# Two graph-attention layers: the column maximum and the raw scores spread by way of memory, and a third of the normalising moved to GpSimd

## The reference

```
h     = relu(layernorm(x))
Wh    = h @ W                              # 1024 x 128
e1,e2 = Wh @ a1, Wh @ a2                   # one number per node each
e     = leaky_relu(e1[i] + e2[j], 0.2)     # 1024 x 1024
att   = softmax over j of e where adj[i, j] > 0
out   = att @ Wh                           # layer 0: elu(out)
x     = x + out
```

## Time and profile before

| | us |
|---|---|
| median of 3 runs | 290.95 (290.85 to 292.67) |
| the profiled execution | 291.18 |
| its span | 289.4 |
| TensorE busy | 285.1 (99%) |
| VectorE busy | 254.4 (88%) |
| ScalarE busy | 195.1 (67%) |
| GpSimd busy | 79.7 (28%) |

### The profile page before, as it was taken

The page is one execution under the profiler, slowest core; times in us unless marked ns, Lnnn a source line. Parts: engine busy times, 40 slices in busy tenths (PEclk is TensorE's granted clock), DMA queues, the critical chain, the costliest instruction groups (busy, mean ns, idle before and its releaser), DMA issues.

```text
span 289.4 us, 6600 instructions
## 1 busy us (share of the span) xinstructions
PE 285.1 (99%) x2523; PEld 284.2 (98%) x2523; DVE 254.4 (88%) x493; ACT 195.1 (67%) x534; POOL 79.7 (28%) x143
## 2 busy tenths in 40 slices
PE   7999999999999999999999999999999999999996
PEld 7999999999999999999999999999999999999995
DVE  3898899898989989898998979979797997779986
ACT  4686795995959679495886929569292865916400
POOL 2412705315071420706035070512407042000000
PEclk9999999999999999999999999999999999999999
DMA  7999659597795949679287896959769596896922
GB/s 235 418 407 407 243 183 408 216 371 298 260 413 163 415 170 359 278 245 412 76 315 286 291 378 204 404 186 389 294 243 410 166 409 250 313 406 205 374 104 75
DMA packets 25387, 84.52 MB, mean 292 GB/s; under 512 B 3966, under 2 KB 5132, under 8 KB 25356
## 3 DMA queue, kind: packets, MB, share of 16 engines
q1 hardware_dynamic: 24780, 83.70, 76.8%
q10 hardware_dynamic: 576, 0.39, 0.4%
HBM read 79.83 MB, written 4.26 MB: 291 GB/s over the span
## 4 chain that ended last, share of the span: by engine, by line
PE 99%; POOL 0%; DVE 0%; issue 0%; POOLq 0%
PE acc L1041 76%; PE prj L957 9%; PE tp L887 5%; PE acc L1056 2%; PE acc L876 2%; PE acc L937 1%; PE tp L976 1%; PE prj L1056 1%; PE prj L927 1%; PE prj L1041 1%; PE tp L970 1%; PE tp L896 0%; PE tp L993 0%; PE tp L985 0%; PE acc L896 0%
## 5 line engine op out<-in xcount | busy, mean ns | idle before, releaser
L1041 PE MATMUL acc<-wh,pbuf 128*128 128x129 f32 x1968 | 227.6, 275 | 0.0
L1041 PEld LDWEIGHTS acc<-wh,pbuf 128*128 128x128 f32 x1968 | 224.0, 192 | 0.1
L734 DVE SCALAR_TENSOR_TENSOR pbuf<-row_r,sqr,adj_sb 128x1024 f32<-128x1024 f32 x125 | 154.8, 1277 | 2.9 <-ACT row_r L483 2.9
L498 ACT ACTIVATE accs<-accs,rec 128x128 f32<-128x128 f32 x120 | 36.6, 388 | 26.7 <-DVE rec L770 26.7
L320 POOL TENSOR_TENSOR mean<-stats 128x8 f32<-128x8 f32 x14 | 11.7, 836 | 142.9 <-DVE stats L632 139.5
L433 ACT ACTIVATE xn<-x_sb,shift,rstd 128x128 f32<-128x128 f32 x120 | 47.7, 479 | 0.0
L466 ACT ACTIVATE wh<-prj,wh 128x128 f32<-128x128 f32 x120 | 32.8, 363 | 0.0
L483 ACT ACTIVATE row_r<-in_row 128x1024 f32<-128x1024 f32 x14 | 29.4, 2098 | 2.4 <-DMA in_row<-row_mem 2.4
L957 PE MATMUL prj<-w_ext,hT 128*128 128x130 f32 x240 | 29.3, 275 | 0.0
L957 PEld LDWEIGHTS prj<-w_ext,hT 128*128 128x128 f32 x240 | 28.0, 191 | 0.0
L347 POOL TENSOR_TENSOR rstd<-vareps,neg_half 128x8 f32<-128x8 f32 x15 | 26.0, 1731 | 6.9 <-DVE vareps L651 5.8
(11 more groups left out here) (114 smaller groups left out, 181.1 us busy)
## 6 DMA issues: line engine op xcount, KB each, us to landing
adj_sb<-in_adj SPq DMA_DIRECT2D x64, 1024.0 KB, 10.7
in_row<-row_mem SPq DMA_DIRECT2D x7, 641.0 KB, 4.3
x_sb<-in_x SPq DMA_DIRECT2D x7, 512.0 KB, 11.5
in_row<-row_mem SPq DMA_DIRECT2D x7, 512.0 KB, 4.3
out_x<-x_sb SPq DMA_DIRECT2D x7, 512.0 KB, 12.9
x_sb<-in_x ACTq DMA_DIRECT2D x1, 256.0 KB, 3.6
x_sb<-in_x SPq DMA_DIRECT2D x1, 256.0 KB, 3.5
row_mem<-sqr SPq DMA_DIRECT2D x14, 4.0 KB
```

What stands on the lines that cost most here:

```text
L498: op = nc.scalar.activation(hp[:, t, :], hp[:, t, :], ACT.Copy, scale=rec[:, t:t + 1])
L734: nc.vector.scalar_tensor_tensor(pbuf[:, t, :], row_r[:, n % 2, :], sqr[:, n % 2, 0, t:t + 1], adj_at(n, t), ALU.max, ALU.min).then_inc(p_ ...
L1041: mm = nc.tensor.matmul(sum_at(k, s), pbuf[:, t, i * P:(i + 1) * P], wh[:, n % 2, t, :], start=(t == 0 and s == 0 and k < NB), stop=(t == ...
```

## The change

Stages 0 and 1 keep their way. From stage 2 on:

- `spread_emax` is no longer called in `attend`. `copy_e_later` puts e1 and e2 in `e_pair`, e1 beside the partition's maximum of e2. `load_row` sends the 128 maxima to memory, then the raw e1, reads the maxima back into every partition (`in_emax`, 128x128), and then the row of e1.
- `exp_args_later` waits for `in_emax`, takes its maximum and makes e2 - c. It stands behind `add_elu` or `add_hp`, ahead of mask 6. `zrow` is gone.
- ScalarE no longer makes r of 8 nodes. `make_row` makes it for 1024 nodes in every partition: Relu(e1 + c) with the sort in it, then Exp in place.
- Q_SCALE * q, the last column of `wh`, is made by GpSimd (`last_column`), and `scale_wh` waits for it.
- GpSimd normalises tiles 5, 6 and 7 (`normalise_pool`), ScalarE tiles 0 to 4.
- `copy_u` goes from ScalarE to VectorE, between `copy_e_later` and mask 2.
- ScalarE's order is the same in both layers: `scale_accs`, elu, `normalise`, `exps_later`, half of `scale_wh`, `make_row`, the other half, `copy_hT`.
- `mask_unsorted` is gone: stage 15 waits for `row_sorted` as others do.

```diff
@@ sync: load_row(m)
+                sp.wait_ge(emax_ready, m + 1)
+                if k > 1:
+                    sp.wait_ge(emax_in, 16 * (k - 1))
+                    sp.wait_ge(row_in, 16 * (k - 1))
+                sp.dma_start(emax_mem[:, :], e_row[:, T:T + 1]).then_inc(emax_written, 16)
+                sp.dma_start(row_mem[0:N].rearrange("(p t) -> p t", t=T),
+                             e_row[:, 0:T]).then_inc(r_written, 16)
...
-                sp.wait_ge(r_known, m + 1)
-                sp.dma_start(row_mem[0:N].rearrange("(p t) -> p t", t=T),
-                             sqr[:, m % 2, 2, :]).then_inc(r_written, 16)
+                sp.wait_ge(emax_written, 16 * k)
+                sp.wait_ge(cmax_ready, m)
+                sp.dma_start(in_emax[:, :], emax_mem.rearrange("p o -> (p o)").partition_broadcast(P)
+                             ).then_inc(emax_in, 16)
                 sp.wait_ge(r_written, 16 * written(m))
@@ gpsimd
+            def normalise_pool(m):
+                pool.wait_ge(shift_ready, m)
+                pool.wait_ge(tr_done, m)
+                src = x3_at(stages[m][1])
+                for t in range(POOL_TILE, T):
+                    nc.gpsimd.tensor_scalar(xn[:, t, :], src[:, t, :], rstd[:, t:t + 1],
+                                            shift[:, t:t + 1], ALU.mult,
+                                            ALU.add).then_inc(xn_pool, 1)
+
+            def last_column(m):
+                pool.wait_ge(q_known, m + 1)
+                nc.gpsimd.tensor_scalar(wh[:, m % 2, :, D], sqr[:, m % 2, 1, :], Q_SCALE, None,
+                                        ALU.mult).then_inc(q_ready, 1)
...
                 normaliser(m)
+                if m > 2:
+                    normalise_pool(m)
+                    last_column(m - 1)
+            last_column(LAST)
@@ scalar
+            def exps_later(m):
+                act.wait_ge(args_ready, m + 1)
+                nc.scalar.activation(sqr[:, m % 2, 1, :], from_max[:, :], ACT.Exp,
+                                     scale=SLOPE).then_inc(q_known, 1)
+                nc.scalar.activation(sqr[:, m % 2, 0, :], from_max[:, :], ACT.Exp,
+                                     scale=1.0 - SLOPE).then_inc(sqr_ready, 1)
...
+            def make_row(m):
                 k = loaded_rows(m)
                 act.wait_ge(row_in, 16 * k)
+                act.wait_ge(cmax_ready, m + 1)
                 act.wait_ge(p_ready, T * (m - 1))
                 nc.scalar.activation(row_r[:, m % 2, :].rearrange("q (t p) -> q t p", t=T),
                                      row_by_node[:, :].rearrange("q (p t) -> q t p", t=T),
-                                     ACT.Copy).then_inc(row_sorted, 1)
+                                     ACT.Relu,
+                                     bias=cmax[:, 0:1]).then_inc(row_added, 1)
+                act.wait_ge(row_added, k)
+                nc.scalar.activation(row_r[:, m % 2, :], row_r[:, m % 2, :], ACT.Exp,
+                                     scale=SLOPE - 1.0).then_inc(row_sorted, 1)
...
                     if n + 2 <= LAST:
-                        normalise(n + 2)
-                    early = T // 2 if elu else T
-                    scale_wh(n + 1, range(early))
-                    sort_row(n + 1)
-                    if early < T:
-                        scale_wh(n + 1, range(early, T))
+                        normalise(n + 2, range(POOL_TILE))
+                    exps_later(n + 1)
+                    scale_wh(n + 1, range(T // 2))
+                    make_row(n + 1)
+                    scale_wh(n + 1, range(T // 2, T))
@@ vector
+            def copy_e_later(m):
...
+                nc.vector.tensor_reduce(e_row[:, T:T + 1], e2, AX_X,
+                                        ALU.max).then_inc(emax_ready, 1)
+            def copy_u(n):
+                k = n // 2
+                dve.wait_ge(upair_done, k)
+                if k > 1:
+                    dve.wait_ge(r_written, 16 * written(n - 1))
+                nc.vector.tensor_scalar(u_sums[:, 0:D], UPAIR, EMPTY, None,
+                                        ALU.mult).then_inc(u_copied, 1)
...
+            def exp_args_later(m):
+                dve.wait_ge(emax_in, 16 * loaded_rows(m))
+                nc.vector.tensor_reduce(cmax[:, :], in_emax[:, :], AX_X,
+                                        ALU.max).then_inc(cmax_ready, 1)
+                dve.wait_ge(cmax_ready, m + 1)
+                nc.vector.tensor_scalar(from_max[:, :], e2, cmax[:, 0:1], None,
                                         ALU.subtract).then_inc(args_ready, 1)
...
                 take_acc(n - 1)
-                copy_e(n + 1)
...
+                copy_e_later(n + 1)
+                if n % 2 == 0:
+                    copy_u(n)
+                masks(n, range(DRAIN, 6))
                 if l == 0:
                     add_elu(b)
+                    exp_args_later(n + 1)
                     masks(n, (6,))
                     add_x(b)
                     masks(n, (7,))
                 else:
                     add_hp(b)
+                    exp_args_later(n + 1)
                     masks(n, (6, 7))
...
-            mask_unsorted(LAST)
-            masks(LAST, range(1, DRAIN))
+            masks(LAST, range(DRAIN))
@@ tensor
             def transposes(m):
+                if m > 2:
+                    pe.wait_ge(xn_pool, (T - POOL_TILE) * (m - 2))
...
-                else:
-                    pe.wait_ge(cmax_ready, m)
...
-                        if t == 0 and i == T // 2 and emax_of is not None:
-                            spread_emax(emax_of)
```

More of the change, by code:

```diff
@@ L37, in gat_two_layers @@
     DRAIN = 2
+    POOL_TILE = 5
     bank_of = [(i // NB, i % NB) for i in range(T)]
@@ L92, in gat_two_layers @@
         ecol = sb("ecol", [P, T, 2])
+        e_pair = sb("e_pair", [P, 2, T + 1])
+        e_row = e_pair[:, 0, :]
+        e2 = e_pair[:, 1, 0:T]
         emax = sb("emax", [P, 1])
@@ L98, in gat_two_layers @@
         row_r = sb("row_r", [P, 2, N])
+        in_emax = sb("in_emax", [P, P])
         in_row = sb("in_row", [P, N + 2 * C])
@@ L118, in gat_two_layers @@
         UPAIR = tp[0:2, BANK:BANK + D]
+        emax_mem = nc.dram_tensor("emax_mem", (P, 1), F32, kind="Internal").ap()
         row_mem = nc.dram_tensor("row_mem", (N + 2 * C,), F32, kind="Internal").ap()
@@ L176, in gat_two_layers @@
         q_ready = sem("q_ready")
+        row_added = sem("row_added")
         row_sorted = sem("row_sorted")
@@ L179, in gat_two_layers @@
         row_in = sem("row_in")
+        emax_written = sem("emax_written")
+        emax_in = sem("emax_in")
+        xn_pool = sem("xn_pool")
         p_ready = sem("p_ready")
@@ L231, in xn_before @@
         def xn_before(m):
-            return T * m - HALF
+            return T * min(m, 3) - HALF + POOL_TILE * max(m - 3, 0)
         block = ctx.enter_context(nc.Block())
@@ L556, in _ @@
                     seed_last()
[L557 to L560, removed]
                 scale_accs(n - 1)
@@ L679, in copy_e @@
                 nc.vector.tensor_copy(ecol[:, 2 * NB:T, :], part).then_inc(e_copied, 1)
-                if m == 1:
-                    nc.vector.tensor_scalar(uniform[:, m % 2, 0:D], USUM, EMPTY, None,
-                                            ALU.mult).then_inc(e_copied, 1)
+                nc.vector.tensor_scalar(uniform[:, m, 0:D], USUM, EMPTY, None,
+                                        ALU.mult).then_inc(e_copied, 1)
                 dve.wait_ge(e_copied, e_copies(m))
                 nc.vector.tensor_reduce(emax[:, :], ecol[:, :, 1], AX_X, ALU.max).then_inc(emax_ready, 1)
+            def copy_e_later(m):
+                dve.wait_ge(prj_done, m + 1)
+                full = prj[:, 0:2, 0:NB * E].rearrange("p b (s e) -> p b s e", e=E)[:, :, :, D:E]
+                nc.vector.tensor_copy(e_pair[:, :, 0:2 * NB].rearrange("p e (b s) -> p b s e", b=2),
+                                      full).then_inc(e_copied, 1)
+                part = prj[:, 2, 0:tiles_in[2] * E].rearrange("p (s e) -> p s e", e=E)[:, :, D:E]
+                nc.vector.tensor_copy(e_pair[:, :, 2 * NB:T].rearrange("p e t -> p t e"),
+                                      part).then_inc(e_copied, 1)
+                dve.wait_ge(e_copied, e_copies(m))
+                nc.vector.tensor_reduce(e_row[:, T:T + 1], e2, AX_X,
[7 more added lines that the diff above has]
+                                        ALU.mult).then_inc(u_copied, 1)
             def exp_args_first():
@@ L701, in exp_args @@
                 nc.vector.tensor_scalar(from_max[:, :], ecol[:, :, 1], cmax[:, 0:1], None,
+                                        ALU.subtract).then_inc(args_ready, 1)
+            def exp_args_later(m):
[4 more added lines that the diff above has]
+                nc.vector.tensor_scalar(from_max[:, :], e2, cmax[:, 0:1], None,
                                         ALU.subtract).then_inc(args_ready, 1)
@@ L736, in masks @@
```

(18 more changed lines are left out.)

8 lines of the change are left out of this document (removed).

## The result

The changed kernel takes 387.15 us (median of 6 runs, 385.46 to 388.37) against 291.07: ratio 1.3285, 95% interval 1.3237 to 1.3334. I had forecast 291.2, and 296.5 at most. From stage 2 on each stage has become 22.5 to 25.1 us long, where it was 17.06 or 17.28.

A forecast was written before the change was run, and what follows sets the result against it. TensorE, busy 285.1 of 289.4 us, was taken as the bound. 291.18 - 1.5 (TensorE) + 0.5 (GpSimd) + 1.2 (end) = 291.4 us profiled, 291.2 against 290.95 by median; range 289.5 to 296.5, the forecast's own 290 to 293.

The forecast's parts named there:

- SyncE's queue: Maxima's trip through memory: write to read 2.3 us, read 1.6, back at C + 4.4, before C + 6.27; no cost.
- C: Moment in each stage when VectorE starts to copy the scores, 2.09 us after `project` begins; stage times count from it.
- rival C: Maxima come after `add_elu`; at the bound C + 7.1, 0.47 us in 13 stages, 6.1: 296.8 us; chance 0.1.
- The step on GpSimd: Normalising three tiles beside masks 2 to 5: done by C + 5.3, holding VectorE 3 x 0.14 = 0.42; 0.5 us in all.
- rival B: GpSimd's operations keep VectorE out their whole length in masks 2 to 5: 4.1 us, 294.8; chance 0.25 with its kin.
- The chain: Work from `add_elu` through arguments, `scale_wh`, `make_row` and hT to `project`: from C + 6.27 to C + 14.5.
- hT's margin: hT, copied last by ScalarE, lets TensorE start `project` at C + 14.5, 0.36 us ahead of need.
- the wait of ScalarE for the column: Before `scale_wh`, ScalarE idles about 1.0 us until GpSimd's `last_column` is done at C + 8.1.
- What leaves TensorE: One transposing instruction in each of 14 stages, 0.11 us each: 1.5 us saved; loop stages at 16.95 and 17.17.
- The end: Stage 15: mask 0 waits for `row_sorted`, first bank free at 273.1, TensorE wants it at 271.96; 1.2 us idle.
- The sum: Whole kernel: 291.18 - 1.5 + 0.5 + 1.2 = 291.4 us for the profiled execution, 291.2 by the median.

The follow-up runs named there:

- e1: Changed kernel with each partition writing 32 bytes (eight numbers) instead of 4, only the first 512 bytes read back; 306.3 us (one run).
- e2: Changed kernel with each partition's 4 bytes written 64 bytes apart, only the first 512 bytes read back; 312.3 us (one run).
- e9: Changed kernel with VectorE turning the column of maxima so that four pieces of 128 bytes are written; 302.83 us, ratio 1.0402 to the kernel before.
- e11: Changed kernel with 16 bytes (four numbers) written per partition instead of 4, only the first 512 bytes read back; 307.7 us (one run).
- e3: Changed kernel with the writes of raw e1 and of the sums issued behind the read of the maxima; 403.2 us (one run).
- e10: e9 with ScalarE normalising all tiles and making the last column, nothing new on GpSimd; 299.26 us, ratio 1.0207 to the kernel before.
- e4: Changed kernel with TensorE spreading the maxima as before instead of the trip through memory; 302.66 us, ratio 1.0415 to the kernel before.
- e8: Kernel before the change with only GpSimd's normalising of three tiles added; 290.93 us, ratio 0.9993.
- e7: e4 with ScalarE normalising all eight tiles and making the last column; 291.64 us, ratio 1.0019 to the kernel before.
- e13: e12 with stage 15 made as in the kernel before, its maxima spread by TensorE; 289.9 us, ratio 0.9972 to the kernel before.
- e12: e10 with one short one-input VectorE instruction put between mask 2 and mask 3; 292.77 us, ratio 1.0057 to the kernel before.
- e5: e4 with ScalarE normalising all eight tiles, GpSimd still making the last column; 292.61 us, ratio 1.0064 to the kernel before.

## Why the prediction was wrong

**The step that failed: "SyncE's queue".** It took the write of the maxima for that of r, "Write to next read took 2.26 us in stage 8", and added 1.6 for the read: C + 4.4. Measured: 8.48 and 5.3 in stage 6, C + 14.2, where "before C + 6.27" was needed. The row I priced by was the same operation in the same place, but of 32 bytes per partition, and the change makes it 4. I bounded the read (by 4.3) and did not bound the write at all. e1 and e2 together show that the price lies in so many pieces lying close together, not in their size or in the queue. The Trainium skill, "DMA: Bandwidth & Descriptors", section "Specifications", names 512 bytes as the least for full rate and has smaller ones read, modified and written back; the pieces of e1, e2, e9 and e11 are all smaller, and take 1.6 to 3.3, so that alone does not give the 8.15. Given the measured write, rival C was the case, at far more than its bound: 14.2 - 6.27 - 0.36 = 7.6 us by stage 6, 98 in 13 stages. The profiled executions have 86 us more in these 13 by the starts of `project` (stage 6 is one of the longer), and 8 more behind the last `project`; the medians differ by 96.

The read was also priced by the wrong row. A store of 64 KB was the nearest in bytes; the read took 5.0 in the changed kernel, 4.0 in e3 and 3.0 to 3.1 in e9 and e10. The row issued behind it does not explain this: in e3 it comes 4 us after the read, in e9 and e10 mostly 0.5 to 1.2 us after it, where the read is shorter. Its cause is open.

**The step on GpSimd** ("three operations, each let in at the end of a mask, end by C + 5.3") was wrong as well, hidden in the changed kernel by VectorE's long waits and worth 10 us in e4. I read L320, let in at the end of one mask, as a rule. In e4, a tile was passed over at the ends of four masks and let in only behind the elu's product. A tile also takes 0.44 us undisturbed, more than the 0.29 that I took for the whole of it. What I did get right is the other direction: the hold on VectorE is small (e8: 0.04 over three masks, 1 us over all 125, against my 0.42 a stage), so rival B has no case. The Trainium skill, "SBUF — State Buffer", section "Who interferes with whom", has the side that comes second wait until the first has finished. By e4 and e10 it waits longer than that: until VectorE runs something other than a two-input instruction, in those stages.

**The chain** was right: 8.27 measured for 8.23, and where nothing starves (e7, e13) `project` is on time. How large hT's margin is, 0.36 or another, no run measures. I had also foretold the wait of ScalarE for the column, about 1.0: the changed kernel has 13.8 us in 14 waits.

**What leaves TensorE** was right: e13 runs at 16.95 and 17.18. **The end** was right in kind and too small: 1.84 us idle in e7 at the first product of stage 15, not 1.2, since the row also came 1.1 us late there. e12 has the wait too:

```profile
272.51 1.41 PEld L1093 LDWEIGHTS acc<-wh,pbuf 128*128 128x128 f32 x12 [2.15 <-issue]
```

Its profiled execution takes 291.71 us and e13's, without the wait, 289.47: 2.24 less, nearly all of it this wait. The rest of the 2.9 between the medians is not in these two traces.

**The sum** without its failed steps stands: 291.4 plus the 1.5 of `spread_emax` is 292.9 by the profiled run, and e5, which is that kernel with the tiles taken off GpSimd, measures 292.61.

Of the signs that I named, the one for rival C came: VectorE's reduction to `cmax` waits for a DMA in all 14 stages. `project` waiting for hT and ScalarE waiting 1 us for the column came with it.

## What to carry to other kernels

When a step is moved to memory, price its transfer by a row with the same bytes per piece and the same spacing, not the same place in the program; where there is none, the write needs an upper bound of its own, and it multiplies by the number of stages. Before many partitions write one number each, turn them into a few rows.

Where GpSimd has work on the path, look at what VectorE does beside it: back-to-back instructions with two inputs in SBUF can shut it out for their whole run if it arrives about when the first of them starts. So leave an opening, and do not queue a short urgent operation behind long ones. Taking an interruption away from VectorE is also a change to GpSimd.

## What the runs showed of the hardware

- 128 writes of 4 bytes into 512 bytes of memory: 8.15 us from issue to the next issue that waits for them, with the DMA engines at 0.00 share for most of it. The same 128 writes 64 bytes apart 3.0, 16 bytes each 3.3, 32 bytes each 3.0, four of 128 bytes 1.6.
- GpSimd's eight-number operation lasts 0.20 us alone, 1.2 to 1.4 us if it gets in at the end of a mask (e12), and up to 6.16 us if it does not (e10). That it gets in between some neighbouring masks and not between others I cannot explain: L320 did before, `shift` does not in e10.
- In stage 6 of the changed kernel TensorE was granted half its clock, 1.2 GHz, for about 3 us after 4.2 us without a product. The profiled executions of e12 and e13, where the longest wait of TensorE is 2.0 us, have the full clock.
